# A graph-attention, GRU and mixture-of-experts layer: the GRU moved one tile behind its attention, the gate two

## What is computed

```python
h = layernorm(x)
Wh = h @ W
e = leaky_relu(Wh @ a[:256] + (Wh @ a[256:]).T, 0.2)
att = softmax(where(adj > 0, e, NEG_INF), axis=1)
h_prime = att @ Wh
gi = h_prime @ w_ih.T + b_ih
gh = h @ w_hh.T + b_hh
r = sigmoid(i_r + h_r); z = sigmoid(i_z + h_z)
n = tanh(i_n + r * h_n)
x = x + (1 - z) * n + z * h
# then: layernorm, a 16-way gate with the top 2 of the softmax,
# silu(x @ w1[e]) * (x @ w2[e]) @ w3[e], weighted and added to x
```

## Time and profile before

| | us |
|---|---|
| median of 3 runs | 1293.75 |
| lowest, highest | 1288.62, 1305.12 |
| the profiled execution, its own time | 1301.45 |
| its span, first to last instruction | 1299.7 |

### The profile page before, as it was taken

The page is one execution under the profiler, slowest core; times in us unless marked ns, Lnnn a source line. Parts: engine busy times, 40 slices in busy tenths (PEclk is TensorE's granted clock), DMA queues, the critical chain, the costliest instruction groups (busy, mean ns, idle before and its releaser), DMA issues.

```text
span 1299.7 us, 25407 instructions
## 1 busy us (share of the span) xinstructions
PE 1189.7 (92%) x7318; PEld 1028.5 (79%) x7319; DVE 1022.7 (79%) x2445; ACT 778.9 (60%) x1141; POOL 347.1 (27%) x351
## 2 busy tenths in 40 slices
PE   5869999999999999999999995269999999999995
PEld 3558888989898989898989893258888888888884
DVE  7744888888888888888888864888887887888883
ACT  2566666666666767676767641026666666666662
POOL 2430111110101011111111100035644644554554
PEclk9869999999999999999999998559999999999998
DMA  7132434343434333333434300142444455435430
GB/s 235 25 65 33 69 59 74 62 72 59 73 59 73 63 69 66 68 68 66 70 62 73 58 13 21 61 130 40 89 98 95 89 148 140 98 94 144 94 49 8
DMA packets 61630, 98.60 MB, mean 76 GB/s; under 512 B 9472, under 2 KB 36096, under 8 KB 61536
## 3 DMA queue, kind: packets, MB, share of 16 engines
q0 software_dynamic: 33600, 52.49, 25.9%
q1 hardware_dynamic: 27936, 44.93, 10.5%
HBM read 213.18 MB, written 18.81 MB: 178 GB/s over the span
## 4 chain that ended last, share of the span: by engine, by line
PE 67%; DVE 15%; ACT 6%; DMA 4%; issue 3%; POOL 2%; DVEq 0%; POOLq 0%; ACTq 0%
PE bank L1212 15%; PE bank L1001 12%; PE bank L1226 9%; PE bank L1119 9%; PE bank L1095 5%; PE bank L1096 5%; PE bank L1097 5%; PE bank L1122 4%; DMA out<-ysc,cidx 3%; DVE pc L734 3%; ACT E L536 2%; ACT pc L482 2%; POOL rs L434 1%; PE bank L1029 1%; DVE scr L768 1%
## 5 line engine op out<-in xcount | busy, mean ns | idle before, releaser
L1095 PE MATMUL bank<-V,pc 128*128 128x258 f32 x1024 | 311.3, 304 | 9.5 <-DVE pc L734 9.5
L1096 PE MATMUL bank<-V,pc 128*128 128x258 f32 x1024 | 291.5, 285 | 0.0
L1097 PE MATMUL bank<-V,pc 128*128 128x258 f32 x1024 | 289.1, 282 | 0.0
L482 ACT ACTIVATE pc<-bank 128x512 fp32r<-128x512 f32 x256 | 152.3, 595 | 170.0 <-PE bank L1001 166.8
L1212 PE MATMUL bank<-wup,xT 128*128 128x512 f32 x948 | 239.6, 402 | 0.9 <-DVE xT L948 0.9
L734 DVE TENSOR_TENSOR pc<-bank,pc 128x512 fp32r<-128x512 f32 x256 | 176.4, 689 | 70.2 <-ACT pc L482 66.1
L1095 PEld LDWEIGHTS bank<-V,pc 128*128 128x128 f32 x1024 | 194.0, 189 | 10.6 <-DVE pc L734 10.6
L1212 PEld LDWEIGHTS bank<-wup,xT 128*128 128x128 f32 x948 | 174.2, 190 | 35.6 <-DVE xT L948 1.3
L1096 PEld LDWEIGHTS bank<-V,pc 128*128 128x128 f32 x1024 | 196.2, 192 | 0.0
L1097 PEld LDWEIGHTS bank<-V,pc 128*128 128x128 f32 x1024 | 196.0, 191 | 0.0
L943 DVE TENSOR_TENSOR wup<-wexp,wup 128x1024 fp32r<-128x1024 f32 x158 | 185.8, 1217 | 2.0 <-ACT wup L482 1.1
(11 more groups left out here) (157 smaller groups left out, 1627.9 us busy)
## 6 DMA issues: line engine op xcount, KB each, us to landing
wexp<-in_L_ffn_w SPq DMA_DIRECT2D x237, 512.0 KB
adjb<-in_adj POOLq DMA_DIRECT2D x128, 256.0 KB, 4.5
token_rows<-xrow SPq DMA_DIRECT2D x32, 130.0 KB, 2.2
E<-in_x SPq DMA_DIRECT2D x8, 512.0 KB, 9.1
xin<-in_x SPq DMA_DIRECT2D x32, 128.0 KB, 2.7
out<-xin SPq DMA_DIRECT2D x32, 128.0 KB, 1.7
xg<-token_rows,gidx POOLq DMA_INDIRECT x79, 3.6
out<-ysc,cidx POOLq DMA_INDIRECT x79, 3.9
```

What stands on the lines that cost most here:

```text
L482: act_copy = lambda o, i: nc.scalar.activation(o, i, ACT.Copy)
L1095: mm(acc[:, 0:VW], hi, V[:, j, 0, :], start=j == 0, stop=False)
L1096: mm(acc[:, 0:VW], hi, V[:, j, 1, :], start=False, stop=False)
L1097: ins = mm(acc[:, 0:VW], lo, V[:, j, 0, :], start=False, stop=j == T - 1)
```

## The change

- **The lags.** The GRU of a tile comes one iteration behind its attention instead of two, the gate two instead of three; `LAST` is T + 2 instead of T + 3. On PE `transpose_h` stands after the slot c = 1, `transpose_x2` and `gru` after c = 2, `gate` after c = 3.
- **The masks.** In the last slots (c = 6 and 7) of iteration i ACT computes the first two quarters of the logits of tile i + 2, and DVE at c = 7 masks the first quarter and subtracts 1 from the second; the other quarters follow at c = 0 to c = 2 of the next iteration. The exponentials stand at c = 2 (two), 3 and 4.
- **Division and remade xn** go from DVE to ACT: DVE keeps the reciprocal (`denominator`), ACT multiplies (`divide`) and computes `xnb` with a per-row scale and bias (`remake_xn`; `nmr` is minus mean times the inverse deviation, made once on DVE). Both stand at the start of ACT's iteration.
- **The end of the GRU.** `gru_out` follows the masks at c = 7; the statistics of the second layernorm stand at the start of DVE's next iteration, ahead of the reciprocal, and the rest of the layernorm behind it.
- **The queues.** SP stores x1 first, then loads the x of tile i (before: of tile i - 1), then stores the row; GpSimd takes the power ahead of the four adjacency loads.

```diff
@@ SP @@
-                if live(i, 1):
-                    v = (i - 1) % 2
-                    if i >= 3:
-                        sp.wait_ge(s_x1, i - 2)
-                    sp.dma_start(xin[:, v, :], x[(i - 1) * P:i * P, :]).then_inc(s_xr[v], 16)
                 if live(i, 2):
                     sp.wait_ge(s_x1, i - 1)
                     sp.dma_start(out[(i - 2) * P:(i - 1) * P, :], x1).then_inc(s_x1s, 16)
+                if live(i, 0):
+                    v = i % 2
+                    if i >= 2:
+                        sp.wait_ge(s_x1, i - 1)
+                    sp.dma_start(xin[:, v, :], x[i * P:(i + 1) * P, :]).then_inc(s_xr[v], 16)
@@ ACT @@
+            def divide(n):
+                act.wait_ge(s_rden, n + 1)
+                if n >= 1:
+                    act.wait_ge(s_th, n)
+                nc.scalar.activation(hp, accs[n % 2][:, 0:F], ACT.Copy, scale=rden[:, 0:1]).then_inc(s_hp, 1)
+
+            def remake_xn(n):
...
+                nc.scalar.activation(xnb[:, v, :], xin[:, v, :], ACT.Identity, scale=rstd[:, n:n + 1],
+                                     bias=nmr[:, n:n + 1]).then_inc(s_xb, 1)
             def body(i):
-                if live(i, 3):
-                    act.wait_ge(s_t2, i - 2)
-                    act_copy(xn2T[:, :, :].rearrange("p k m -> p (k m)"), tp[:, 0:F]).then_inc(s_t2e, 1)
-                if i + 1 < T:
-                    for q in range(Q):
-                        logits(i + 1, q)
+                if live(i, 1):
+                    divide(i - 1)
+                    remake_xn(i - 1)
                 for c in range(CPT):
                     if live(i, 0):
                         chunk_hi(i * CPT + c + 2)
-                    if 1 <= c < 1 + Q and i + 1 < T:
+                    if c < 2 and i + 1 < T:
+                        logits(i + 1, c + 2)
+                    if c == 1 and live(i, 1):
+                        copy_hT(i)
+                    if c == 2 and live(i, 2):
+                        copy_x2T(i + 1)
+                    if c == 2 and i + 1 < T:
+                        weights(i + 1, 0)
+                        weights(i + 1, 1)
+                    if 3 <= c < 5 and i + 1 < T:
                         weights(i + 1, c - 1)
+                    if c == 4 and live(i, 1):
+                        rz_tanh(i + 1)
+                    if c == 5 and live(i, 2):
+                        gate_exp(i + 1)
+                    if c == 5 and live(i, 1):
+                        n_tanh(i + 1)
+                    if c >= 6 and i + 2 < T:
+                        logits(i + 2, c - 6)
@@ DVE @@
+            def denominator(n):
                 dve.wait_ge(s_mm, (n + 1) * CPT)
-                acc = accs[n % 2]
-                link(V_.reciprocal(rden[:, :], acc[:, F:F + 1]))
                 if n >= 1:
-                    dve.wait_ge(s_th, n)
-                V_.tensor_scalar(hp, acc[:, 0:F], rden[:, 0:1], None, ALU.mult).then_inc(s_hp, 1)
+                    dve.wait_ge(s_hp, n)
+                V_.reciprocal(rden[:, :], accs[n % 2][:, F:F + 1]).then_inc(s_rden, 1)
             def body(i):
                 ahead = i + 1 < T
...
+                if live(i, 2):
+                    norm2_statistics(i)
                 if live(i, 1):
-                    combine(i - 1)
-                    remake_xn(i - 1)
...
+                    denominator(i - 1)
+                if live(i, 2):
+                    norm2(i)
                 for c in range(CPT):
                     if live(i, 0):
                         chunk_lo(i * CPT + c + 2)
                     if c == 0 and ahead:
+                        mask_logits(i + 1, 1)
+                        less_one(i + 1, 2)
+                    if c == 2 and ahead:
+                        mask_logits(i + 1, 2)
+                        less_one(i + 1, 3)
                         mask_logits(i + 1, 3)
                         row_max(i + 1)
...
+                    if c == 7 and i + 2 < T:
+                        less_one(i + 2, 0)
+                        mask_logits(i + 2, 0)
+                        less_one(i + 2, 1)
+                    if c == 7 and live(i, 1):
+                        gru_out(i + 1)
@@ PE @@
             def body(i):
-                if live(i, 3):
-                    transpose_x2(i)
-                if live(i, 2):
-                    gru(i)
...
-                    if c == 0 and live(i, 3) and live(i, 0):
-                        gate(i)
-                    if c == 3 and live(i, 1):
+                    if c == 1 and live(i, 1):
                         transpose_h(i)
+                    if c == 2 and live(i, 2):
+                        transpose_x2(i + 1)
+                    if c == 2 and live(i, 1):
+                        gru(i + 1)
+                    if c == 3 and live(i, 2):
+                        gate(i + 1)
```

More of the change, by code:

```diff
@@ L265, in gnn_moe @@
         block = ctx.enter_context(nc.Block())
-        LAST = T + 3
+        LAST = T + 2
         def live(i, lag):
@@ L350, in body @@
                     sp.dma_start(out[(i - 2) * P:(i - 1) * P, :], x1).then_inc(s_x1s, 16)
-                if live(i, 3):
-                    sp.wait_ge(s_row, i - 2)
-                    sp.dma_start(rows[(i - 3) * P:(i - 2) * P, :], xrow[:, (i - 3) % 2, :]).then_inc(s_rows[(i - 3) % 2], 16)
+                if live(i, 0):
[4 more added lines that the diff above has]
+                if live(i, 2):
+                    sp.wait_ge(s_row, i - 1)
+                    sp.dma_start(rows[(i - 2) * P:(i - 1) * P, :], xrow[:, i % 2, :]).then_inc(s_rows[i % 2], 16)
             for i in range(LAST):
@@ L563, in _ @@
             chunk_hi(1)
+            logits(1, 0)
+            logits(1, 1)
             def rz_tanh(i):
@@ L597, in body @@
                             weights_step(n)
[L598 to L603, removed]
-                    if c == 4 and live(i, 3):
-                        gate_exp(i)
             for i in range(LAST):
@@ L828, in _ @@
             link(V_.tensor_tensor(bias_rz[:, :], bias_rz[:, :], bhh_rz, ALU.add))
+            V_.scalar_tensor_tensor(out=nmr[:, :], in0=xmv[:, :, 0], scalar=-1.0, in1=rstd[:, :], op0=ALU.mult,
+                                    op1=ALU.mult).then_inc(s_nmr, 1)
             chunk_lo(0)
             chunk_lo(1)
+            less_one(1, 0)
+            mask_logits(1, 0)
+            less_one(1, 1)
             def body(i):
                 ahead = i + 1 < T
-                if ahead:
-                    less_one(i + 1, 0)
-                    less_one(i + 1, 1)
+                if live(i, 2):
+                    norm2_statistics(i)
                 if live(i, 1):
-                    combine(i - 1)
-                    remake_xn(i - 1)
-                if ahead:
-                    mask_logits(i + 1, 0)
-                    less_one(i + 1, 2)
-                    mask_logits(i + 1, 1)
-                    less_one(i + 1, 3)
-                    mask_logits(i + 1, 2)
+                    denominator(i - 1)
+                if live(i, 2):
+                    norm2(i)
                 for c in range(CPT):
@@ L1151, in body @@
             def body(i):
-                if live(i, 3):
-                    transpose_x2(i)
-                if live(i, 2):
-                    gru(i)
-                if live(i, 3) and not live(i, 0):
-                    gate(i)
                 for c in range(CPT):
```

47 lines of the change are left out of this document (24 added, 23 removed).

## The result

The changed kernel takes 1384.3 us, the median of four runs (1380.5 to 1390.9), against 1293.2 us for the kernel before (four runs, 1288.6 to 1305.1). The ratio is 1.068, with a 95% interval of 1.061 to 1.076: slower by 91 us. The forecast was 1369 us, slower. The profiled execution took 1380.69 us (span 1378.9) against 1301.45 (span 1299.7), which is 79 us more, where the forecast's sum said 75.

A forecast was written before the change was run, and what follows sets the result against it. PE was taken to bound the old kernel (21.86 us an iteration), a closed chain of 24.85 the new one. 29 iterations add 87 us, the ends -4 and -8, together +75: from 1293.75 to 1369 us, range 1340 to 1395.

The forecast's parts named there:

- What bounds the old kernel: Middle of the attention: PE bounds the 21.86 us iteration with 21.24 of work; only one 0.62 us stop is gainable.
- DVE's queue ahead of the reciprocal, 4.69 us: DVE, after the last chunk_lo: masks, subtractions, GRU's end, statistics and the reciprocal itself sum to 4.69 us before the division.
- The three waits of PE, 2.4, 0.4 and 0.8: PE waits each iteration before transpose_h (2.4 us), slot 2's accumulation (0.4) and the xrow transposes (0.8), 3.6 in all.
- ACT's two operations, 0.39 and 0.48: Division and remade xn, moved to ACT, take 0.39 and 0.48 us there, including per-row operands.
- The rival of dearer operations: ACT's division and remade xn cost 0.48 and 0.66 us, +0.27 each iteration, 1377 us; chance 0.03.
- The closed chain, 24.85 an iteration: Links over PE, ACT and DVE close to a cycle of 24.85 us, the new iteration length instead of PE's 21.24.
- The clock at 1.00: PE keeps the full granted clock in the attention despite three stops, 3.6 us in all, each iteration.
- The rival with the clock: Clock falls for the GRU products: 5 us more in each of 30 iterations, about 1520 us; chance 0.04.
- The ends, -4 and -8: Up to tile 2 saves 4 us (0 to 7); last tile's first accumulation to its one-hots saves 8 (4 to 11).
- The sum: Whole program: +87 us over 29 iterations, -4 and -8 at the ends, together +75.
- An earlier settling: DVE and ACT settle earlier in the iteration: iterations of 24.2 us, +56, 1350 us; chance 0.15.
- PE's pace: No late results for PE: iterations of 21.24 us, 1264 us, faster than before; chance 0.05.

The follow-up runs named there:

- e9: e8 with the second layernorm on DVE moved ahead of the mask, statistics right behind the reciprocal; 1270.9 us, ratio 0.979 to the kernel before.
- e2: Changed kernel with the reciprocal ahead of the second layernorm's statistics on DVE; 1355.98 us.
- e3: Changed kernel with the reciprocal ahead of both the GRU's end and the layernorm statistics on DVE; 1353.72 us.
- e5: e2 with the next tile's first mask and its subtractions also moved behind the reciprocal on DVE; 1346.68 us.
- e10: Changed kernel with 20 extra identity transposes on PE before transpose_h waits for the quotient; median 1376.8 us, ratio 1.062 to the kernel before.
- e4: Changed kernel with division and remade xn back on DVE, behind the reciprocal; median 1352.8 us, ratio 1.041 to the kernel before.
- e7: Changed kernel with only ACT's order new: division behind two chunk copies and third logits, hT copy next, remade xn earlier; iteration 23.06 us.
- e11: e6 with layernorm statistics right behind the reciprocal and the rest behind slot 2's chunk_lo, ahead of the mask; iteration 23.56 us.
- e1: Changed kernel with the hT copy ahead of the fourth logits on ACT; one run, 1377.05 us.
- e6: Changed kernel with only DVE's order new: first mask before the last chunk_lo, reciprocal first, statistics and layernorm later; iteration 24.02 us.
- e8: Changed kernel with the new DVE order of e6 and the new ACT order of e7 together; 1284.9 us, ratio 0.986 to the kernel before.

## Why the prediction was right, and where its sizes were off

**What bounds the old kernel: right.** Nothing but the 0.62 us stop could be won from PE, and e9, which removes all stops, ends at 21.25 against the 21.24 that was added up.

**DVE's queue ahead of the reciprocal, 4.69 us: right.** From the last `chunk_lo`'s successor (309.63) to the division's start (314.36) are 4.73, and e2, e3 and e5, which take work out of it, shorten the undisturbed iteration by 0.9, 1.4 and 1.4.

**The three waits of PE, 2.4, 0.4 and 0.8: right.** The idle times are 2.28, 0.35 and 0.65, which with 21.24 make only 24.52. An idle time begins at the end of the last product as the profile has it, though; the prediction counts by starts. By starts, against e9, where the same instructions on PE have no stop:

```profile
345.55 0.60 PE L1031 MATMUL bank<-ident,E 128*128 128x128 f32 x4
347.43 0.38 PE L1031 MATMUL bank<-ident,scr 128*128 128x128 f32 x2
348.22 0.37 PE L1125 MATMUL bank<-V,pc 128*128 128x258 f32 x1
349.76 0.39 PE L1031 MATMUL bank<-ident,xrow 128*128 128x128 f32 x2
```

these are 1.88, 0.79 and 1.54 between the four rows. The kernel after has 4.31, 1.17 and 2.36 (311.11, 315.42, 316.59, 318.95), so 2.43, 0.38 and 0.82 more, in all 3.63.

**ACT's two operations, 0.39 and 0.48: right.** To their successors they take 0.37 and 0.49; their lengths are 0.47 with one operand per row and 0.59 with two, against 0.40 without. The Trainium skill ("ScalarE: Activation LUTs", section "What ACT_TABLE_LOAD costs") says some 93 ns for each such operand; the lengths show 0.07 for the first and 0.19 for both, and so agree within 0.02. The rival of dearer operations falls.

**The closed chain, 24.85 an iteration: right.** Undisturbed iterations take 24.91, and all of e10's do. The undisturbed iterations of six variants came within 0.1 of what the chain gave for them (e2, e3, e4, e5, e7, e11). Three missed: e1 by 0.3 (24.53 against 24.8), e6 by 0.4 and e8 by 0.3, these two with the long power.

**The clock at 1.00: this step failed.** I read from the earlier trace rows that PE could work 2.25 of 4 us and keep the full clock, and applied this one case, a stop of 2.08 us, to a stop that returns in each iteration. The same trace has the other case too: in the stop of 5.88 of the earlier trace rows the clock is at 0.50 from 90 to 91, before PE works again at 91.67. The mean iteration became 25.24 instead of 24.91. From the first accumulation of tile 2 to that of tile 31 are 732.6 us (132.52 to 865.13), against 633.7 before: +98.9, where the sum had +87. Of the 12 missing, 10 are the clock (0.35 on 29 iterations) and 2 the undisturbed iteration, 24.91 instead of 24.85. The share of 86% for PE became 90 for the same reason; the undisturbed iteration has 88. The rival with the clock had 0.04 and priced it at 5 us an iteration; it came true in part, at a fourteenth of that price.

**The ends, -4 and -8: right.** Up to the first accumulation of tile 2 the change gains 2.9 us (135.46 to 132.52); the third accumulation of the first tile now waits less, as said of the earlier trace rows:

```profile
87.04 0.39 PE L1125 MATMUL bank<-V,pc 128*128 128x258 f32 x1 [1.95 <-DVE pc L764]
```

From the first accumulation of the last tile to the end of its one-hots are 41.0 us (865.13 to 906.12; 40.6 forecast, 48.9 before):

```profile
905.75 0.37 DVE L821 TENSOR_SCALAR pick<-iota_e,xrow 128x16 bf16<-128x16 f32 x2
```

**The sum.** -2.9 + 98.9 - 7.9 = +88.1 at that row (818.06 to 906.12), against the +75 forecast. The spans differ by only 79.2 because the profiled run of before lost 8.9 us more after it, nearly all in the experts and the last writes, which the change does not touch. The error of the forecast is therefore 13 us in the attention, and the profiled pair hides most of it; the medians, 91 apart, show it. Carrying the sum over to the median by subtracting 7.7, the distance of the profiled run of before from its median, fits this: 1301.45 + 88.1 - 7.7 is 1382, and 1384.3 was measured. That the other runs of before were shorter in their experts is not shown, since only one was profiled.

**The rivals.** An earlier settling (24.2) and PE's pace (21.24) are refuted by the iterations read; that PE's pace can be had with these lags was left open, and e9 shows that it can (1270.9 us, where the rival had 1264), by an order in which neither DVE nor ACT has anything long between the last accumulation and what PE waits for.

## What to carry to other kernels

When work is moved between engines or iterations, lay one iteration out on all queues from measured starts, follow what each queue holds ahead of the result that the next engine waits for, and see whether the links close to a cycle: its length, not the busiest engine, is the new period. Put the short operation on which another engine waits first in its queue and the long independent ones behind it; here the reciprocal first saved 0.9 us an iteration (e2), and both queues laid out anew by this rule (e9) turned a loss of 7% into a gain of 2%, with the same instructions. And where a stop of the TensorE returns in each iteration, leave room in the forecast for a clock that falls after it, and read the granted clock in windows of 1 us before calling it unharmed.

## What was not expected of the hardware

**A small GpSimd operation is stretched by a long DVE one.** The power on 128x1 took 1.53 us when it started 0.11 to 0.13 us into a mask of 1.23 us (28 times of 32 in e6 and in e8), and 0.56 beside a `chunk_lo` (e9, e11); no other kernel here has it start during a mask, and in none is it longer than 0.57. Between e6 and e11 lie 0.46 us an iteration, between e8 and e9 0.40. The Trainium skill ("SBUF — State Buffer", section "Who interferes with whom") says that a DVE instruction with two inputs in SBUF contends with a GpSimd instruction that reads SBUF, for a pair of ports that it calls an exclusive lock. The trace agrees: the mask reads `E` and `adjb`, `chunk_lo` reads one input from a bank, and the power of 1.53 ended at 305.85, 0.43 after the mask (305.42), a little less than the 0.56 that it takes undisturbed.

**The clock falls to half after a stop of 2.3 us in some iterations only.** With the longest stop at 2.28 us (the kernel after) the iterations lie between 24.90 and 25.86; with 1.34 (e7) all are 23.05 to 23.09. e2, with 1.40, has four of 26 at 24.4 to 24.7 and the others at 24.03 to 24.07; e4, with 2.11, has a granted clock of 0.98 to 1.00 in the windows of 100 us from 150 to 750, e3, with 2.03, 0.98 in all, and e5, with 0.34 and 1.44, 0.98 and once 0.97. So the length of the longest stop alone does not order them. What picks the iterations was not tried and stays open.

**The rest of the program has its own scatter.** In the preparation, the profiled runs of e7 and e8 had a granted clock of 0.59 from 40 to 80 us, where before had 0.79 and 0.73, and their first accumulation came at 91.8 and 91.6 instead of 78.6. Neither touches the attention's iterations. Without distances read inside the stage that was changed, effects under some 10 us would have been put down to the wrong cause.
